# A decoder layer on one core: the order of its first 28 microseconds rewritten

## The reference

```
x = x + attn(layernorm(x))     # 16 heads: causal 4-tap convolution of q and k, silu, layer norm per head,
                               # gated delta-like recurrence S = (1-b) S + b v k^T, o = S q, times silu gate, Wo
x = x + xattn(layernorm(x), ctx_1024)   # softmax((ctx Wq + bq)(ctx Wk + bk)^T) mixes the tokens of layernorm(x)
x = x + ffn(layernorm(x))      # 16 routed experts (top 4 of 2 groups) and a shared one
```

## Time and profile before

| what | value |
|---|---|
| median of 3 runs | 582.71 us (580.95 to 583.91) |
| the profiled execution's own time | 582.77 us |
| its span, first to last instruction | 581.0 us |
| TensorE busy | 556.8 us (96% of the span) |
| VectorE, ScalarE, GpSimd busy | 433.4, 398.3, 292.8 us |
| mean granted TensorE clock | 0.991 |

### The profile page before, as it was taken

The page is one execution under the profiler, slowest core; times in us unless marked ns, Lnnn a source line. Parts: engine busy times, 40 slices in busy tenths (PEclk is TensorE's granted clock), DMA queues, the critical chain, the costliest instruction groups (busy, mean ns, idle before and its releaser), DMA issues.

```text
span 581.0 us, 9944 instructions
## 1 busy us (share of the span) xinstructions
PE 556.8 (96%) x3392; PEld 487.5 (84%) x3392; DVE 433.4 (75%) x1046; ACT 398.3 (69%) x782; POOL 292.8 (50%) x194
## 2 busy tenths in 40 slices
PE   3898999999999999999999999989799999999997
PEld 1687889989989899899899898877678888888887
DVE  7768998998998899889989988977867543323333
ACT  3978888879778789798797887785653333333431
POOL 2335656656567467466565674420201565556552
PEclk9998999999999999999999999999799999999999
DMA  6032032031030230230211202210100532343221
GB/s 208 23 120 83 0 120 83 1 118 61 24 119 12 72 119 2 82 105 16 83 57 63 83 1 101 82 30 2 55 1 0 168 126 82 111 128 126 86 88 72
DMA packets 18001, 42.31 MB, mean 73 GB/s; under 512 B 4736, under 2 KB 6528, under 8 KB 17952
## 3 DMA queue, kind: packets, MB, share of 16 engines
q1 hardware_dynamic: 17952, 41.69, 21.4%
HBM read 40.47 MB, written 1.21 MB: 72 GB/s over the span
## 4 chain that ended last, share of the span: by engine, by line
PE 88%; ACT 4%; DVE 4%; issue 1%; DMA 1%; SPq 0%; DVEq 0%; ACTq 0%
PE bank L1346 21%; PE bank L1348 20%; PE bank L1347 20%; PE bank L1342 16%; PE bank L1483 5%; PE bank L1471 4%; ACT tok L671 2%; DMA xbias<-in_xb 1%; DVE stats L1051 1%; PE bank L1357 1%; PE bank L1550 1%; ACT values L585 1%; DVE x L1336 0%; DVE raw L1070 0%; DVE xT_lo L986 0%
## 5 line engine op out<-in xcount | busy, mean ns | idle before, releaser
L1346 PE MATMUL bank<-xT_lo,w_hi 128*128 128x512 f32 x320 | 133.7, 418 | 1.9 <-DVE conv L1070 1.2
L1348 PE MATMUL bank<-xT_hi,w_hi 128*128 128x512 f32 x320 | 126.1, 394 | 0.0
L1347 PE MATMUL bank<-xT_hi,w_lo 128*128 128x512 f32 x320 | 125.6, 392 | 0.0
L464 POOL TENSOR_TENSOR gated_lo<-gated,gated_hi 128x512 fp32r<-128x512 f32 x30 | 38.7, 1291 | 116.4 <-ACT gated_hi L691 112.7
L671 ACT ACTIVATE tok<-bank,nmr,rstd 128x128 f32<-128x128 f32 x256 | 91.3, 504 | 2.0 <-DVE nmr L966 2.0
L1346 PEld LDWEIGHTS bank<-xT_lo,w_hi 128*128 128x128 f32 x320 | 60.5, 189 | 16.1 <-DVE conv L1070 3.2
L459 POOL TENSOR_TENSOR conv<-tap,conv 128x506 f32<-128x506 f32 x32 | 61.9, 1935 | 21.7 <-DVE conv L1070 21.7
L459 POOL TENSOR_TENSOR raw<-tap,raw 128x506 f32<-128x506 f32 x32 | 61.9, 1936 | 20.3 <-DVE raw L1070 16.3
L1348 PEld LDWEIGHTS bank<-xT_hi,w_hi 128*128 128x128 f32 x320 | 60.3, 189 | 13.5
L1051 DVE BATCH_NORM_STATS2 stats<-bank 128x6 f32<-128x128 f32 x256 | 56.3, 282 | 16.3 <-PE bank L1471 16.3
L1347 PEld LDWEIGHTS bank<-xT_hi,w_lo 128*128 128x128 f32 x320 | 60.7, 190 | 9.1
(11 more groups left out here) (184 smaller groups left out, 1403.6 us busy)
## 6 DMA issues: line engine op xcount, KB each, us to landing
obet<-obet_rows SPq DMA_DIRECT2D x16, 768.0 KB, 4.4
w_raw<-in_w SPq DMA_DIRECT2D x22, 384.0 KB, 4.6
tap<-route_rows SPq DMA_DIRECT2D x16, 512.0 KB, 3.9
w_raw<-in_w SPq DMA_DIRECT2D x12, 256.0 KB, 2.9
wv_raw<-in_wv SPq DMA_DIRECT2D x8, 256.0 KB, 4.9
wo_raw<-in_wo SPq DMA_DIRECT2D x8, 256.0 KB, 5.0
w_raw<-in_w SPq DMA_DIRECT2D x12, 128.0 KB, 2.1
x<-in_x SPq DMA_DIRECT2D x2, 512.0 KB, 4.7
```

The lines of the kernel that those rows point to most:

```text
L464: nc.gpsimd.tensor_tensor(gated_lo[:, cc], gated[:, c * N:(c + 1) * N], gated_hi[:, cc].bitcast(F32), ALU.subtract).then_inc(gated_lo_read ...
L1346: nc.tensor.matmul(o, l_hi, r_lo, start=start, stop=False, skip_group_check=loose)
L1347: nc.tensor.matmul(o, l_lo, r_hi, start=False, stop=False, skip_group_check=loose)
L1348: return nc.tensor.matmul(o, l_hi, r_hi, start=False, stop=stop, skip_group_check=loose)
```

## The change

- x comes in four loads instead of two, with a semaphore each; the statistics wait for theirs.
- The three context loads are issued from ScalarE's queue instead of SyncE's.
- The memsets of dmask and obetT are done by GpSimd (semaphore zeros_ready), not by VectorE.
- GpSimd's first split waits for VectorE's four norm copies (ln_norm_dve) instead of for rstd.
- On VectorE the eight copies into dmask stand behind the low parts of x and wb.
- On ScalarE norm's copies and the transposes' copies come right behind the first weight copy; the copies of values' weights and of wb come after them, and the four context outputs stand between the taps and ahead of the second weight copy.
- On TensorE the third context product goes behind the transposes, the fourth behind the first projection.

```diff
--- before.py
+++ after.py
@@ -251,7 +251,7 @@
 
         ld = {n: sem("ld_" + n) for n in
               ("const", "tie", "ctx", "beta", "router", "obet", "wo", "obet_rows", "route_rows", "out")}
-        ld_x = [sem(f"ld_x{i}") for i in range(NCH)]
+        ld_x = [sem(f"ld_x{i}") for i in range(TT // 2)]
         ld_w = [sem(f"ld_w{i}") for i in range(2)]
         ld_down = [sem(f"ld_down{i}") for i in range(2)]
         ld_prm = [sem(f"ld_prm{i}") for i in range(G)]
@@ -281,6 +281,7 @@
             sem("b_full"), sem("b_ready"), sem("b_tok_full"), sem("b_tok_ready"))
         b_lo_ready, r_lo_ready = sem("b_lo_ready"), sem("r_lo_ready")
         obet_ready, dmask_ready = sem("obet_ready"), sem("dmask_ready")
+        zeros_ready = sem("zeros_ready")
         r_full, r_score = sem("r_full"), sem("r_score")
         r_tok_full, r_tok_ready = sem("r_tok_full"), sem("r_tok_ready")
         r_ready, r_tr_full, r_tr_ready = sem("r_ready"), sem("r_tr_full"), sem("r_tr_ready")
@@ -294,11 +295,8 @@
 
         @block.sync
         def _(sp):
-            for c in range(NCH):
-                sp.dma_start(x[:, c * T:(c + 1) * T], x_in[:, c * T:(c + 1) * T]).then_inc(ld_x[c], 16)
-            sp.dma_start(xw, xw_in).then_inc(ld["ctx"], 16)
-            sp.dma_start(ctxT, ctx_in).then_inc(ld["ctx"], 16)
-            sp.dma_start(xb[:, :], xb_in).then_inc(ld["ctx"], 16)
+            for u in range(TT // 2):
+                sp.dma_start(x[:, u * N:(u + 1) * N], x_in[:, u * N:(u + 1) * N]).then_inc(ld_x[u], 16)
             sp.dma_start(ident[:, :], ident_in).then_inc(ld["const"], 16)
             sp.dma_start(wb, wb_in).then_inc(ld["beta"], 16)
             sp.dma_start(bb, bb_in).then_inc(ld["beta"], 16)
@@ -470,8 +468,10 @@
                 nc.gpsimd.tensor_tensor(wo_lo[:, w], wo_raw[:, :], wo_hi[:, w].bitcast(F32),
                                         ALU.subtract).then_inc(wo_lo_ready, 1)
 
-
-            pool.wait_ge(ln_rstd, NCH)
+            nc.gpsimd.memset(dmask[:, :], 0.0).then_inc(zeros_ready, 1)
+            nc.gpsimd.memset(obetT, 0.0).then_inc(zeros_ready, 1)
+
+            pool.wait_ge(ln_norm_dve, 2 * NCH)
             split_low(0, 0)
             low_values(0, 0)
             split_low(0, 1)
@@ -600,8 +600,10 @@
                 nc.scalar.activation(attT[:, u * N:(u + 1) * N], bank[4 + u][:, :], ACT.Identity,
                                      bias=xb[:, u // NCH:u // NCH + 1]).then_inc(x_qk_ready, 1)
 
-            act.wait_ge(ld["beta"], 32)
-            nc.scalar.activation(wb_hi, wb, ACT.Copy).then_inc(small_split, 1)
+            act.dma_start(xw, xw_in).then_inc(ld["ctx"], 16)
+            act.dma_start(ctxT, ctx_in).then_inc(ld["ctx"], 16)
+            act.dma_start(xb[:, :], xb_in).then_inc(ld["ctx"], 16)
+
             def high(g, k):
 
                 s = k % 2
@@ -698,18 +700,21 @@
                 nc.scalar.activation(wo_hi[:, w], wo_raw[:, :], ACT.Copy).then_inc(wo_hi_ready, 1)
 
             high(0, 0)
+            for c in range(NCH):
+                half_norm(0, c)
+            for c in range(NCH):
+                half_out(0, c, xT_hi)
             act.wait_ge(ld_wv[0], 16)
             nc.scalar.activation(wv_hi[:, 0:N], wv_raw[:, 0:N], ACT.Copy).then_inc(wv_hi_ready, 1)
+            act.wait_ge(ld["beta"], 32)
+            nc.scalar.activation(wb_hi, wb, ACT.Copy).then_inc(small_split, 1)
+            first_taps(0, 0, (0,))
             context_out(0)
             context_out(1)
-            for c in range(NCH):
-                half_norm(0, c)
+            first_taps(0, 0, (1,))
             context_out(2)
-            for c in range(NCH):
-                half_out(0, c, xT_hi)
             context_out(3)
             high(0, 1)
-            first_taps(0, 0, (0, 1))
 
             for c in range(NCH):
                 act.wait_ge(b_full, c + 1)
@@ -986,28 +991,26 @@
                     nc.vector.tensor_tensor(xT_lo[:, cc], bank[2 * c + kt][:, :], xT_hi[:, cc].bitcast(F32),
                                             ALU.subtract).then_inc(ln_split, 1)
 
-            obet_zero = steps.did(nc.vector.memset(obetT, 0.0))
-            a = steps.did(nc.vector.memset(dmask[:, :], 0.0))
-
             for t in range(TT):
-                dve.wait_ge(ld_x[t // G], 16)
+                dve.wait_ge(ld_x[t // 2], 16)
                 ins = x_stats(t)
             steps.after(steps.did(ins))
             norm_factors(TT, D).then_inc(ln_rstd, NCH)
             for c in range(NCH):
                 half_norm(0, c)
 
+            for c in range(NCH):
+                half_low(0, c)
+            dve.wait_ge(small_split, 1)
+            nc.vector.tensor_tensor(wb_lo, wb, wb_hi.bitcast(F32), ALU.subtract).then_inc(b_lo_ready, 1)
+
             dve.wait_ge(ld["const"], 16)
-            steps.after(a)
+            dve.wait_ge(zeros_ready, 1)
             dm = dmask[:, :].rearrange("p (b c) -> p b c", b=B)
             for b in range(B):
                 nc.vector.tensor_copy(dm[:, b, 0:P], ident[:, :])
                 ins = nc.vector.tensor_copy(dm[:, b, L:L + P], ident[:, :])
             ins.then_inc(dmask_ready, 1)
-            for c in range(NCH):
-                half_low(0, c)
-            dve.wait_ge(small_split, 1)
-            nc.vector.tensor_tensor(wb_lo, wb, wb_hi.bitcast(F32), ALU.subtract).then_inc(b_lo_ready, 1)
 
             def context_max(e):
                 dve.wait_ge(x_energy, e + 1)
@@ -1106,7 +1109,7 @@
             taps(0, 0, 1)
 
             dve.wait_ge(b_ready, NCH)
-            steps.after(obet_zero)
+            dve.wait_ge(zeros_ready, 2)
             bt = betaT.rearrange("h (b t) -> h b t", b=B)
             ob = obetT.rearrange("h (b c) -> h b c", b=B)
             nc.vector.tensor_scalar(ob[:, :, 1:L], bt[:, :, 1:L], -1.0, 1.0, ALU.mult,
@@ -1368,10 +1371,9 @@
             context_qk(0)
             context_qk(1)
             pe.wait_ge(ld["const"], 16)
-            context_qk(2)
             for c in range(NCH):
                 half_transpose(0, c)
-            context_qk(3)
+            context_qk(2)
 
             def energies(b):
                 if b < 2:
@@ -1556,6 +1558,7 @@
             project_in(0, 0, 0, (0,))
             pe.wait_ge(ln_split, KT * NCH)
             project_in(0, 0, 0, (1,))
+            context_qk(3)
             beta_logits()
             project_in(0, 0, 1)
             beta_tokens()
```

## The result

The changed kernel takes 586.64 us (median of 4 runs, 586.41 to 588.20), the kernel before 582.07 beside it (4 runs, 580.95 to 583.91): a ratio of 1.008 [1.0052, 1.0108], **slower by 0.8%**. Its profiled execution took 586.41 us with a span of 584.6, so 3.6 us more than that of before. TensorE's share of the chain that ended last is 86% [before: rows 1]. The front tells where the time went.

A forecast was written before the change was run, and what follows sets the result against it. The prediction took ScalarE to bound the front, with TensorE holding 88% of the chain that ended last. It summed 582.77 + 0.3 (later gate projection) + 1.6 (TensorE's clock) = 584.7 us, range 581.3 to 586.9.

The forecast's parts named there:

- the clock: TensorE behind T: a gap of 3.3 us idle drops its clock to about half speed, costing +1.6 us.
- T: TensorE's start of head 0's first gate projection, where before and after meet: forecast 28.15 against 27.83, +0.3 us.
- the landing of x: Last quarter of x, loaded beside the context: forecast at 7.8 us, bounds 6.55 and 8.6.
- B: End of ScalarE's two sigmoids, taken to set T: forecast 25.05 us against 24.54 before.
- rival A: Clock also down at the front's transposes: +1.5 us, in all 586.2 us; chance 0.20.
- A: Start of ScalarE's norm copies, once rstd is ready: forecast 11.0 us, bounds 10.5 and 11.8.
- C: End mark defined with the results: ScalarE begins the next conv on TensorE's release; 32.38 us before, 35.92 changed.
- B = A + 14.05: Sum of ScalarE's rows from norm copies to the sigmoids' end in the new order, giving 25.05 us.
- T = B + 3.1: From the sigmoids' end to the first gate projection: 3.1 us, against 3.29 before, giving 28.15 us.
- P: Start of TensorE's first projection: forecast 15.05 us, 2.5 us earlier than 17.57.
- Rival B: No clock loss ahead of the gate projection, as the beta transposes keep it up: 583.1 us; chance 0.23.
- Rival C: TensorE's earlier start at the first projection goes through to the end: 2.5 us less, 580.3 us; chance 0.12.

The follow-up runs named there:

- second runs: The changed kernel run once more, unedited, with a second profile, beside the kernel before: 587.36 us, ratio 1.010.
- e1: Changed kernel with the three context loads back on SyncE's queue, behind the four x loads: 587.62 us, 1.0108 of the kernel before.
- e7: Changed kernel with the loads of before (x in two, then context, all on SyncE's queue): 586.36 us, 1.0079 of the kernel before.
- e3: Changed kernel with the four context outputs moved from between the first taps to behind taps 2 and 3: 583.71 us, 1.0036 of the kernel before.
- e5: Changed kernel with GpSimd's taps 0 and 1 ahead of its second split: 587.33 us, 1.0091 of the kernel before.
- e4: Changed kernel with twelve unread matmuls on TensorE ahead of the gate projection: 585.64 us, 1.0072 of the kernel before.
- e10: e7 with twelve unread matmuls on TensorE ahead of the gate projection: 583.39 us, 1.0037 of the kernel before.
- e6: Kernel before with the new loads, memsets on GpSimd and GpSimd's wait, but the old order on ScalarE, TensorE and VectorE: 582.76 us, 1.0015.
- e9: Kernel before with only the last two context outputs moved behind the two gates: 580.50 us, 0.9987 of the kernel before.
- e8: e7 with GpSimd's taps 0 and 1 before its second split, context outputs behind taps 2 and 3 and each gate: 583.61 us, 1.0034.

## Why the prediction was right and wrong

The direction held, the range just so (586.64 with an upper end of 586.9; the second runs' median is 587.36), and of the mechanism ScalarE as the bound and the fall of the clock. The size did not hold: +1.9 us was forecast, +3.6 is in the profile and +4.6 between the medians. The sum was 0.3 for T and 1.6 for the clock. At T 1.1 came on top from the landing of x and 0.9 from the held decay row, less 0.15 at B, which gives the 2.2 measured; the clock took 1.4. So it is in part luck that the range held: it was wide for rival A and for 0.7 us at the landing, and what filled it were a landing beyond its bound and a row that counted for nothing. By its own steps:

- *The landing of x*: taken at 7.8 with 8.6 as the upper bound; it was about 8.8, and the factors came at 12.11 for 11.0. **This term failed**, with its upper bounds for the landing (8.6) and for A (11.8). The prediction asked only what shares the engines and let the four loads cost nothing: e1 shows 1.0 for these alone. Nor was the context through early: its products were to end at about 10.7 and ended at 12.03, as its last load landed at 8.25. The Trainium skill, "DMA: Bandwidth & Descriptors", section "Issuing engines are not separate DMA queues", says that the DMAs of all issuing engines run on the same 16 DMA engines and interleave. The prediction's estimate from it, 8.4 for the landing, was nearer than the value taken. Yet the time hardly depends on this term: e1 and e7 have the factors 1.3 and 1.7 us earlier, C only 0.3 and 0.6 earlier, and lose as much by their ratios.
- *B = A + 14.05*: 13.90. ScalarE as the bound of the front and the sum of its rows held, e3's 2.2 us for the four outputs too. In e7, with A at 10.76, B is 24.89 where 24.81 follows.
- *T = B + 3.1*: 4.0. **This is the other step that failed.** The prediction asked when GpSimd's results are needed and called its part nothing, though it had read the held norm copies from the earlier trace rows. The new order puts ScalarE's second weight copy behind four outputs, so GpSimd's second split and the taps behind it slide from 19.03 and 22.41 to 23.52 and 25.32, beside the decay rows. The second row is held by the late tap. e5 moves the taps away and gets 1.1 back at T. The break-even at A = 10.5 was wrong by the same: e7's T is 28.88, where 27.9 follows from the sum.
- *The clock*: 3.3 us idle ahead of T and +1.6. TensorE idles 0.66 and 3.28 us there, as T is later, and the clock fell; it costs 1.37 in the changed kernel's first profile (e4), 1.93 in e7 (e10) and, by T to C, 2.7 in the second profile. The 3.3 us at half speed behind the 1.6 stand in no row of before, whose rows show only a fall by 46.7 that is over by 50.8; here the half speed holds from T, 30.0, to 33.1. Rival B, no fall of the clock, is out.
- *TensorE's early start is worth nothing*: P came 1.5 us earlier (2.5 forecast) and went whole into the gap. e6 starts its projections 1.2 later than the changed kernel and ends first. Rival C is out.
- *Rival A* is no rival but an addition: in some executions the transposes are slow and 1.8 us come on top (1.5 forecast). It is one reason why the changed kernel's times can part by more than the first profiles do. How often it happens isn't settled.
- *Memsets, waits, issues on ScalarE*: nothing; memsets of 1.38 and 1.37 us from 0.74 on, and e6 as a whole within 0.27%. The memsets alone were not tried.

The chance for slower by over 0.5% was 0.22 and too small: the held row could only make T later and stood in no term, and the upper bound of the landing was too low.

Open is a part of the medians. The two later falls of the clock account for some of it: the traces of before and of the changed kernel have both, so their 3.6 us compare like with like, but the trace of before (582.77) is slower than its kernel's median of 581.13 to 582.07, while that of the changed kernel (586.41) lies at its kernel's 586.64. e10's C is 1.0 later than before's and its median 2.3 later. What makes the later falls come and go, and whether the front bears on it, was not tried.

## What to carry to other kernels

Work on the bounding engine that fills the wait for a late input is free there; put behind the input it is on the path. Before moving it, look which engine's time is used up between the input and the next meeting point, and move filler into waits that come later instead, as e9 does. An engine that gets its work earlier without its next partner doing so only gets a longer gap, and on TensorE such a gap is paid again in clock. And when VectorE and GpSimd share a stretch, list what stands beside what after a move, since the engine that nobody waits for can hold the one that all wait for.

## What the runs showed of the hardware

- A VectorE row from SBUF to SBUF beside a GpSimd operation takes the latter's time as well: 1.46 for 0.40, four norm copies 3.87 for 1.38, the low part of wb 0.95 for 0.18. The first decay row starts beside a GpSimd operation in all fourteen traces, the one of before too, and always ends 0.54 to 0.55 us after that operation does, whether it takes 0.83 (e5), 1.09 (before) or 2.08 (e8). In the changed kernel GpSimd's second tap is longer too, 1.69 for 1.25. The Trainium skill, "SBUF — State Buffer", "Who interferes with whom", says that VectorE in a mode that uses two ports contends with GpSimd: the one that issues first keeps the shared ports for its whole instruction and the other blocks. The held rows start inside GpSimd's operations and end shortly behind them, so the trace agrees; which mode VectorE was in no run shows.
- Ahead of T the clock fell after gaps of 3.28, 2.20 and 1.76 us (e5 and e8 the last two) and not after 1.19 nor, in e3, after 1.85. So a gap's length alone doesn't decide it in this range. A fall made T to C 1.4 to 2.7 us longer (5.92 to 7.21 against 4.55).
- Later falls, near 46 to 55 and 410 to 423 us, come in some executions and not in others; each goes with about 1.5 us.
- The same sixteen transposes at the front took 2.03 or 3.65 us in two executions of one kernel, at a granted clock shown as 1.00.
- Four loads of x in place of two, with the context loads behind them on the same queue, had the last one there 1.0 us later (7.51 in e1 against 6.55).
